# Expert gate of a four-layer network as plain fp32 products of 64-column halves, from a whole copy of the turned rows

## What is computed

```python
x = x + _L0_conv_ref(_ln_c(x), ...)       # window attention
t = t + _L0_ffn_ref(_ln_t(t), ...)        # feed-forward with binarised weights
x = x + _L1_conv_ref(_ln_c(x), ...)       # attention in 8x8 windows
t = t + _L1_ffn_ref(_ln_t(t), ...)        # experts
x = x + _L2_conv_ref(_ln_c(x), ...)       # Fourier mixer
t = t + _L2_ffn_ref(_ln_t(t), ...)        # experts
x = x + _L3_conv_ref(_ln_c(x), ...)       # Fourier mixer with routed filters
t = t + _L3_ffn_ref(_ln_t(t), ...)        # experts
```

```python
scores = jnp.einsum('bsd,de->bse', x, gate_w) + gate_b
probs = jax.nn.softmax(scores, axis=-1)
topk_vals, topk_idx = jax.lax.top_k(probs, TOP_K)
mask = jnp.sum(jax.nn.one_hot(topk_idx, NUM_EXPERTS, dtype=probs.dtype), axis=-2)
masked = probs * mask
masked = masked / (jnp.sum(masked, axis=-1, keepdims=True) + 1e-09)
h = jax.nn.gelu(jnp.einsum('bsd,edh->ebsh', x, w1) + b1[:, None, None, :], approximate=False)
y = jnp.einsum('ebsh,ehd->ebsd', h, w2) + b2[:, None, None, :]
out = jnp.einsum('bse,ebsd->bsd', masked, y)
```

## Time and profile before

| | before |
|---|---|
| median of three runs | 855.95 us (853.36, 855.95, 859.4) |
| the profiled execution | 852.62 us, span of the trace in it 850.8 us |
| PE busy | 758.4 us (89%) |
| PE weight loads | 617.3 us (73%) |
| DVE busy | 589.0 us (69%) |
| ACT busy | 435.6 us (51%) |
| POOL busy | 561.4 us (66%) |
| chain that ended last | PE 71%, DVE 12%, POOL 7%, issue 5%, ACT 4% |
| in that chain, by line | L1779 22%, L1752 8%, L1753 7%, L1756 3%, L1475 3%, L1763 1% |

### The profile page before, as it was taken

One profiled execution on the slowest core, in us unless ns is written; L12 is line 12 of the kernel. 1 busy time (PEld: TensorE's weight loads), 2 busy tenths in 40 slices (PEclk: granted clock), 3 DMA queues, 4 the chain that ended last, 5 costly groups with the idle time before them and its releaser, 6 DMA issues.

```text
span 850.8 us, 27655 instructions
## 1 busy us (share of the span) xinstructions
PE 758.4 (89%) x10695; PEld 617.3 (73%) x10695; DVE 589.0 (69%) x1604; ACT 435.6 (51%) x792; POOL 561.4 (66%) x888
## 2 busy tenths in 40 slices
PE   3897657499899999969997999999969999999996
PEld 2666546377678888857876688888858876888886
DVE  6687539678757777747885377777877773777754
ACT  3674545367554444438774445344446655444441
POOL 4655533455287888768764488878667784888764
PEclk9697569789999999989999999999979999999999
DMA  6711100000221111000002011011000010110030
GB/s 154 141 12 30 35 1 1 2 4 3 64 70 30 41 44 29 2 2 1 0 13 64 1 56 32 28 29 30 3 1 2 1 30 28 43 46 29 28 86 20
DMA packets 39513, 26.23 MB, mean 31 GB/s; under 512 B 27499, under 2 KB 32348, under 8 KB 39412
## 3 DMA queue, kind: packets, MB, share of 16 engines
q1 hardware_dynamic: 38444, 24.46, 11.4%
q10 hardware_dynamic: 968, 0.38, 0.2%
HBM read 7.92 MB, written 1.57 MB: 11 GB/s over the span
## 4 chain that ended last, share of the span: by engine, by line
PE 71%; DVE 12%; POOL 7%; issue 5%; ACT 4%; POOLq 0%; DVEq 0%; ACTq 0%
PE PS L1779 22%; PE PS L1752 8%; PE PS L1753 7%; PE PS L1756 3%; PE PS L1475 3%; PE PS L1854 2%; PE PS L1867 2%; PE PS L1887 2%; PE PS L1878 2%; PE PS L1897 2%; PE PS L1568 2%; POOL H L558 2%; PE PS L1763 1%; DVE X L1271 1%; POOL rs L501 1%
## 5 line engine op out<-in xcount | busy, mean ns | idle before, releaser
L748 ACT ACTIVATE H<-PS,B 128x512 f32<-128x512 f32 x288 | 173.7, 691 | 193.9 <-PE PS L1756 193.9
L1779 PEld LDWEIGHTS PS<-M,H 128*64 128x64 f32 x4608 | 192.4, 137 | 21.6 <-issue 19.4
L1779 PE MATMUL PS<-M,H 128*64 128x96 f32 x4608 | 205.2, 248 | 1.8 <-DVE X L1271 1.8
L1271 DVE SCALAR_TENSOR_TENSOR X<-PS,G,X 128x96 f32<-128x96 f32 (+1 forms) x384 | 121.8, 318 | 96.5 <-PE PS L1779 86.2
L487 POOL TENSOR_TENSOR msum<-stats 128x4 f32<-128x4 f32 (+1 forms) x61 | 16.6, 272 | 104.6 <-DVE stats L931 88.2
L497 POOL TENSOR_TENSOR XN<-X,mean 128x384 f32<-128x384 f32 x56 | 47.6, 850 | 47.6 <-PE PS L1475 47.6
L1752 PE MATMUL PS<-XH,M1h 128*128 128x512 f32 x192 | 77.9, 406 | 0.0
L1753 PE MATMUL PS<-FHL,M1l 128*128 128x512 f32 x192 | 76.1, 397 | 0.0
L523 POOL TENSOR_TENSOR PF<-G,B 128x1536 f32<-128x1536 f32 x24 | 66.2, 2759 | 10.2 <-DVE G L1262 10.2
L531 POOL TENSOR_TENSOR ex<-euler,dl 128x16 f32<-128x16 f32 x24 | 69.8, 2909 | 1.7 <-DVE dl L1235 1.6
L501 POOL TENSOR_TENSOR rs<-ve,half 128x4 f32<-128x4 f32 (+1 forms) x61 | 66.1, 1084 | 4.8
(11 more groups left out here) (251 smaller groups left out, 1735.1 us busy)
## 6 DMA issues: line engine op xcount, KB each, us to landing
FHL<-XH SPq DMA_DIRECT2D x36, 192.0 KB, 2.5
FHL<-XL SPq DMA_DIRECT2D x36, 64.0 KB, 2.1
X<-XH SPq DMA_DIRECT2D x12, 192.0 KB, 2.5
raw<-L_ffn_w SPq DMA_DIRECT2D x3, 576.0 KB, 4.9
M<-L_ffn_w SPq DMA_DIRECT2D x3, 576.0 KB, 4.8
XH<-XL SPq DMA_DIRECT2D x24, 64.0 KB, 1.9
out<-X SPq DMA_DIRECT2D x8, 192.0 KB, 2.5
X<-x SPq DMA_DIRECT2D x3, 384.0 KB, 6.4
```

What stands on the lines that cost most here:

```text
L748: act.activation(H[p][:, c, :], bank(UB[c]), ACT.Gelu, bias=B1[e][:, c:c + 1]).then_inc(gelu_a, 1)
L1271: ins = dve.scalar_tensor_tensor(xt(g, t), bank(4 + t % 2)[:, e * C:(e + 1) * C], G[:, t, e:e + 1], xt(g, t), ALU.mult, ALU.add)
L1779: ins = pe.matmul(Y[rows, x * C:(x + 1) * C], H[p][:, j, t * P + rows.start:t * P + rows.stop], M2[e][:, j, :], start=c == 0, stop=c == CH ...
```

## The change

The gate no longer uses the split halves. ACT makes an unrounded fp32 copy of the turned rows (`whole_gate`), and the gate is one plain fp32 product of this copy with the original four columns GWr of weights, per tile in two halves of 64 stationary columns, as `down` has them. Per group that is eight product instructions as before, without sums over several of them.

The copy goes to one of two buffers by turns: xv0, or a part of PT (a buffer of the attention). It waits for `lo_v` of the same group (the rest XL is computed) and for the gate that read the buffer before. It stands on ACT behind the fourth gelu of a body, at the opening of each expert stage, and once in the second attention, the last body of the second and that of the third mixer. Since it reads bank 7, what writes that bank next has to wait for it: PE waits for `xv_a` ahead of the next turn, ahead of chunk 11 (chunk 5 in the opening), and of course ahead of the gate. The gate's output has four columns per tile instead of eight, L1231 goes, and so do GW, its two casts per layer, and the memsets that zeroed the bias of the low half. The counts on `split_v` shift accordingly.

The diff, cut to its core:

```diff
-        GP = PS[:, 4, EXP * C:EXP * C + GT * 2 * EXP]
+        GP = PS[:, 4, EXP * C:EXP * C + GT * EXP]
...
+        XW = [xv0[0:C, :], PT[:].rearrange("p h t -> p (h t)")[0:C, GT * HEADS * 64:GT * HEADS * 64 + GTOK]]
...
+            def whole_gate(m, p):
+                act.wait_ge(lo_v, m + 1)
+                act.wait_ge(xt_used, m - 1)
+                act.activation(XW[p], turned(m), ACT.Copy).then_inc(xv_a, 1)
...
+                    if ka == 1 and g == GROUPS - 2:
+                        whole_gate(m + 2, p)
                     if has(g, 1):
                         act.wait_ge(sub_v, n + 2)
                         act.activation(SC[:, 0:GT * HEADS * bs], SC[:, 0:GT * HEADS * bs], ACT.Exp).then_inc(exp_a, 1)
...
                 def body(g, p):
+                    if opening(g):
+                        whole_gate(8 * k + 1, 1)
                     if has(g, 1):
                         gelus(8 * e + g + 1, 1 - p, 0, 3)
                     if has(g, 2, 2, PREPS[phase]):
                         prep_hi(8 * k + g + 2, p, CK * (8 * e + g + 1))
                     if has(g, 1):
-                        gelus(8 * e + g + 1, 1 - p, 3, CK)
+                        gelus(8 * e + g + 1, 1 - p, 3, 4)
+                    if has(g, 2, 2):
+                        whole_gate(8 * k + g + 2, p)
+                    if has(g, 1):
+                        gelus(8 * e + g + 1, 1 - p, 4, CK)
...
             def mixer2(g, p):
                 if has(g, 1):
                     mix_relu(0, 3, g)
+                if isinstance(g, int) and g == GROUPS - 1:
+                    whole_gate(32, 0)
                 if has(g, 2, 2, PREPS[4]):
                     prep_hi(24 + g + 2, p)
...
                 halves(M1h[i][0:C], M1l[i][0:C], raw[0:C], EW[i])
-                halves(GW[i][0:C, 0:EXP], GW[i][0:C, EXP:], GWr[i][0:C], EW[i] + 2)
...
                 dve.tensor_tensor(gs[:], GP.rearrange("p (t e) -> p t e", t=GT),
-                                  GBr[b_layer][:].unsqueeze(1).to_broadcast([P, GT, 2 * EXP]), ALU.add).then_inc(gate_v, 1)
-                dve.wait_ge(gate_v, NGV * b + 1)
-                sc = gs[:, :, 0:EXP]
-                dve.tensor_tensor(sc, sc, gs[:, :, EXP:], ALU.add).then_inc(gate_v, 1)
+                                  GBr[b_layer][:].unsqueeze(1).to_broadcast([P, GT, EXP]), ALU.add).then_inc(gate_v, 2)
+                sc = gs[:]
...
                         if c == 11 and turned is not None:
                             pe.wait_ge(lo_v, turned)
+                            if copied is not None:
+                                pe.wait_ge(xv_a, copied)
...
                     after(pe, gate_v, NGV * b - NGV + 1)
+                    pe.wait_ge(xv_a, b + 17)
                     for t in range(GT):
-                        ts, o = slice(t * P, (t + 1) * P), 2 * t * EXP
-                        pe.matmul(GP[:, o:o + 2 * EXP], XH[p][0:C, ts], GW[e][0:C], start=True, stop=False)
-                        ins = pe.matmul(GP[:, o:o + EXP], XL[p][0:C, ts], GW[e][0:C, 0:EXP], start=False, stop=True)
+                        for rows in HALF:
+                            ins = pe.matmul(GP[rows, t * EXP:(t + 1) * EXP], XW[p][:, t * P + rows.start:t * P + rows.stop], GWr[e][0:C],
+                                            start=True, stop=True)
...
                     if has(g, 2, 2, PREPS[phase]):
+                        pe.wait_ge(xv_a, b + 18)
                         prep_turn(m + 2, extra=(gelu_a, CK * (b + 1) + (1 if has(g, 1) else 0)))
...
                 if has(g, 2, 2, PREPS[4]):
+                    if isinstance(g, int) and g == GROUPS - 1:
+                        pe.wait_ge(xv_a, 25)
                     prep_turn(24 + g + 2)
```

31 lines of the change are left out of this document (17 added, 14 removed).

## The result

| | before | after |
|---|---|---|
| median | 856.14 us (four runs, 853.36 to 859.4) | 844.26 us (four runs, 842.91 to 845.58) |
| profiled execution | 852.62 us, span 850.8 | 845.14 us, span 843.3 |
| PE busy | 758.4 us | 750.5 us |
| PE weight loads | 617.3 us | 610.3 us |
| DVE busy | 589.0 us | 550.9 us |

The ratio of the timed runs is 0.9888, with a 95% interval of 0.9845 to 0.9931: 9.6 us faster (5.9 to 13.3), where the prediction said 8.9 less than before and 847.0 us.

A forecast was written before the change was run, and what follows sets the result against it. PE, busy throughout the expert stages, was taken as the bound. −9.4 − 0.28 − 0.28 + 1.0 + 0.1 = −8.9 us on the profiled 852.62 gave 843.7, or 847.0 against the timed median 855.95; range 842 to 855.5.

The forecast's parts named there:

- What PE loses and gets: At the gate, 0.70 instead of 1.15 us from last "down" load to first "up" load: gain 0.45 us a gate.
- the entry: From the last "down" load to the gate's first load: 0.08 us.
- the exit: From the gate's last load to the first "up" load, across the change of tiles: 0.21 us.
- Rival A: At the gate, a pair of halves keeps 0.081 us: 0.24 us gained a gate, sum −4.5, 851.4 us; chance 0.20.
- rival B: The gate's 16 loads go one after another: nothing gained on PE, sum +0.5, 856.5 us; chance 0.10.
- How often it counts: In the expert stages 21 gates count, all but those of the opening bodies: 21 × 0.45 = −9.4 us.
- DVE and POOL: In the gating head, removing L1231 (2.16 us, a wait ending with POOL's L523) counts nothing; removed casts were counted too.
- the two casts: Removed gate-weight casts: −0.28 us in front of the first expert stage, −0.28 in the second mixer, third pair nothing.
- ACT's copies: 24 copies of 0.59 us: nothing in the groups, +1.0 us ending the second mixer, +0.1 ending the second attention.
- the end of the second mixer: PE's turn for group 33 waits for ACT's copy of group 32, which stands behind the spectrum: +1.0 us.
- Rival C, the clock: Second mixer's end: idle before the late turn drops PE to 1.2 GHz, five blocks lose 4.5: 851.5 us; chance 0.06.
- the two cases that held 0.45 and 0.46: For the whole time, chance 0.45 of faster and 0.46 of the same, with the bound at one per cent, 8.6 us.

The follow-up runs named there:

- grouped order: The changed kernel with the gate's four lower halves of all tiles issued first, then the four upper ones: 851.76 us, ratio 0.9989.
- 128 columns: The changed kernel with the gate as one plain fp32 product of 128 columns per tile instead of two of 64: 854.23 us, ratio 1.0022.
- second profile of the change: The changed kernel measured and profiled once more, unaltered: ratio 0.9896 to the kernel before, profiled execution 839.43 us.
- copies alone: The kernel before plus ACT's 24 unrounded copies and their waits; gate, weights' halves and DVE's work as before: ratio 0.9996.
- turn behind the gate: The changed kernel with PE's turn in the expert stages moved from between the two "down" products to behind the gate: 874.76 us, ratio 1.0262.
- quarters: The changed kernel with the gate's products in four quarters of 32 stationary columns per tile instead of two halves of 64: 842.12 us, ratio 0.9885.

## Why the prediction was right, point by point

*What PE loses and gets.* Right, and nearly to the hundredth. Predicted 0.70 us from the last "down" load to the first "up" load, measured 0.68; a pair every 0.058, measured 0.059; the entry 0.08, measured 0.08; from the gate's first load to its last 0.41, measured 0.44; the exit 0.21, measured 0.16. That the last two misses have opposite signs is luck, though a small one. The gain is 0.47 to 0.48 us a gate instead of 0.45. Rival A (0.081 a pair) and rival B (one after another, 16 x 0.058) are out by the rows. The estimate worked because a pair was priced as one load of 64 columns, and the slope from 96 to 128 columns gave that load. The Trainium skill (TensorE: Matmul & The Clock Gate, section The mechanism) says that a weight load overlaps products in flight only where the row groups differ, from which the prediction drew rival B. The measurement decides against that here: the halves share their rows, and a pair takes the time of one load (0.059 us). In the grouped order the loads of the same half follow one another every 0.058 us.

*How often it counts.* Right for 20 of the 21: they show 0.478 us each in the two traces, and with 128 columns 10.4 us came back. The second gate of the first expert stage gives less, since PE waits for DVE there: from turn 18 to 19 it takes 17.90 us with 128 columns and 17.58 in the second profile of the change, 0.32 us.

*DVE and POOL.* Right that L1231's wait is POOL's and costs nothing either way. Of the two casts, the one of the second mixer is worth 0.25 us as predicted (0.28). The one in front of the first expert stage was mis-sized: the stretch from turn 18 to 19 is 18.03 us before and 17.90 with the changed DVE but a gate as dear as before ("128 columns"), 0.13 us. The wait at the second gate, 0.83 us before, is 0.70 in the second profile of the change. DVE's start is not all that this wait hangs on; what else was not followed. Together, from turn 17 to 19, that gate and this cast brought 0.36 us (40.33 before, 39.97 in the second profile of the change), where the prediction had 0.45 and 0.28.

*ACT's copies.* In the groups right: the copy ran 262.30 to 262.89, 0.70 us behind XL, and the next two gelus were done at 264.05, 1.86 us behind XL, as worked out (1.9); PE shows no wait for a copy in any group. At the end of the second mixer the chain came as told and cost 1.08 us (predicted 1.0), measured with the copies alone. At the end of the second attention the copy cost nothing: from turn 16 to 17 it is 5.69 us after and 5.70 before (predicted +0.1).

*Rival C, the clock.* It was looked for in the wrong place. The idle of 1.46 us in front of the late turn did not bring the clock down. But the next idle behind it, 3.35 us long in both kernels, did so at another moment, and the clock came back about 4 us earlier: 1.6 us gained in both profiles of the change, which more than pays for the copy there. Two of the eight profiles with the copy at this place didn't have that gain, so it is not a sure part of the change. The prediction treated the stretch behind L1867 as fixed; it is not. The price of an idle is not settled by its length either: behind idles of 1.50, 1.50 and 1.66 us the clock fell in three groups of the kernel with the turn behind the gate, and behind others of up to 1.60 us it did not.

*The sum.* 20 x 0.478 = 9.6 for the gates, 0.36 for the twenty-first and the cast ahead of it, 0.25 for the other cast, less the copy's 1.08: 9.1 us from the change's own parts, where the prediction had 8.9. With the clock's 1.6 it is 10.7; the timed ratio says 9.6 with an interval of 5.9 to 13.3, the second call 8.9 (5.9 to 11.9). These intervals confirm the size of the whole, but none of the terms under 1 us; those rest on the rows alone. The profiled pair alone (7.5 us and, with the second profiles, 12.9) would have told too little or too much by what the clock did: of the 12.9, 1.6 lie behind the copy and 2.1 in the third mixer (95.49 to 93.35), and the rest is the 9.1.

*The chances.* The result lies just beyond 1%, with an interval of 0.7 to 1.6% across the bound between the two cases that held 0.45 and 0.46. The range of 842 to 855.5 held the median of 844.26. That median lies 2.7 us below the forecast of 847.0; the change's own parts explain 0.2 of that and the clock behind the copy, for which the prediction had nothing, about 1.6.

## What to carry to other kernels

Here products that stream only 4 or 8 columns cost what their weight loads cost, and two 64-column halves issued by turns cost one load of 64 columns together; but a tile shape unlike that of the products ahead of it gave 0.2 us back at the change (0.27 us from load to load for quarters, 0.08 for halves). So it is worth trying to give small products their neighbour's shape and to put them beside it. Before such a piece is moved, follow what is released by it on the other engines: here a turn that stood one "down" and a gate later (about 2.6 us, 260.55 to 263.10 above) cost more than all that halves had gained. And where PE's clock falls in stretches with idle time, two profiles of one kernel may differ by more than the change under study: compare stretch by stretch, and count on those where PE is busy throughout.
